# A convolution's weights arrive turned and early, and its 64-wide groups are spread over the four quadrants of the array

## The chip, the core and the metric

The kernel runs on one core of a Trainium2 chip. TensorE (PE) multiplies matrices and writes PSUM; VectorE (DVE), ScalarE (ACT) and GpSimd (POOL) do elementwise work, POOL only in SBUF; SyncE (SP) starts most DMA transfers. Each engine works through its own list of instructions in order, and they wait for each other by semaphores. The metric is the device time of one execution in microseconds (us).

## The reference, cut to what matters

Two layers, each an attention `s` and a gated network `g`, with `x = x + s * g`. The change is in the first layer, on 2 x 1024 tokens of 512 channels.

```
xn = layernorm(x)
# gate: g = silu(layernorm(relu(xn@up)**2 @ down + routed(xn)) * gamma + beta)
qkv = xn @ w_qkv.T                      # q 1024, k 256, v 256 channels
q = conv(q, qc1_w, qc1_b, groups=16)    # causal, 3 taps, 64 channels a group
k = conv(k, kc1_w, kc1_b, groups=4)     # the same, 4 groups
q = conv(q, qc2_w, qc2_b, groups=1);  k = conv(k, kc2_w, kc2_b, groups=1)
q += 0.5 * mean over heads of k_pre;    k += 0.5 * mean over heads of q_pre
... l2norm, rope, softmax attention, w_o
```

In the "first convolution" an output channel reads only the 64 channels of its own group, at three token positions.

## The kernel before, in words

The program is a row of phases, and between two phases all engines meet at a barrier.

**Gate phase** (names `a_`): four chunks of 512 tokens. Of each chunk DVE normalises x, PE transposes it to xnT, SP stores xnT to memory, PE makes the hidden, latent and output products, DVE and POOL do the second layernorm, ACT does the silu and stores g. Into a large buffer that is free at that time (`conv_in`) SP also loads the weights of the next phase as they lie in memory; the grouped ones go into blocks of 128x128 that POOL has zeroed (L280).

**Preparation** (a block of its own, L434 to L526): PE transposes 90 blocks of 128x128 weights (L450), ACT and DVE copy them to `b_wT`, `b_c1T`, `b_kc1T`, `b_kc2T`. ACT and DVE also measure the weights (sums of squares and of magnitudes, L474 to L496) for a bound on the size of the convolved q, from which a scale is worked out (L502 to L514), and DVE sums the weights over heads (`b_mean`, `b_meanT`, L520, L525). All this ends before the next block starts.

**Projection phase** (names `b_`, from L540): four rounds (2 batches x 2 halves of 512 tokens), each of 25 units. A unit is a group of matmuls into one of five PSUM banks, which ACT (even units) or DVE (odd units) empties ("takes"). Units 0 to 9 make q and k (4 matmuls of 128x512 each, L624). Units 10 to 19 are the first convolution, 8 for q and 2 for k: three matmuls, one a tap, with a 128x128 weight block in which two 64x64 groups stand on the diagonal and the rest is zero (L629). Then 2 units of v, one of the means, 2 of the second convolution of k. The q units are taken with scale and bias to one of two buffers `b_convs`, from which POOL makes a high and a low half-precision part in `conv_in` (L609, L611); a take waits until POOL is done with the buffer of two units before. The matmuls are float32, and the trace shows two MATMUL records for each (one for a transpose).

The query phase (names `c_`) then begins with DVE reading weights (L1045).

Of the kernel before, what the change touches and what calls it, by code (L numbers as in the profile page):

```python
# [9 lines left out]
ALU = mybir.AluOpType  # L10
# [53 lines left out]
def gate_phase(nc, sem, dram, ident, half, weights):  # L64

    with ExitStack() as ctx:
# [6 lines left out]
        up = sb("up", [P, KD, INT])  # L73
        down = sb("down", [P, MI, D])
# [6 lines left out]
        x_in = sb("x_in", [P, TT, D])  # L81
# [10 lines left out]
        g_out = sb("g_out", [P, TT, D])  # L92
# [40 lines left out]

        UNITS = MI + ML + 1 + ML
# [5 lines left out]
        def _(sp):  # L140
            sp.dma_start(x_in[:], x_rows[0]).then_inc(x_loaded, 16)
            sp.dma_start(ident[:], dram["ident"]).then_inc(w_loaded, 16)
            sp.dma_start(up[:], dram["up_w"].rearrange("(k p) n -> p k n", p=P)).then_inc(w_loaded, 16)
# [3 lines left out]
            sp.dma_start(down[:], dram["down_w"].rearrange("(k p) n -> p k n", p=P)).then_inc(w2_loaded, 16)  # L147
# [3 lines left out]

            weights.load(sp)
            sp.wait_ge(weights.zeroed, 1)
            weights.load_pairs(sp)
# [5 lines left out]
            for c in range(NCH - 1):  # L160
                sp.wait_ge(xn_ready, c + 1)
                sp.dma_start(x_in[:], x_rows[ds(c + 1, 1)].rearrange("a p t d -> p (a t) d")).then_inc(x_loaded, 16)
                store(c)
            store(NCH - 1)
# [52 lines left out]
        def _(act):  # L217
# [25 lines left out]
            def silu(c):  # L243
                act.wait_ge(g_stored, 16 * (c + 1))
                for t in range(TT):
                    act.wait_ge(shifted, c * TT + t + 1)
                    act.activation(g_out[:, t, :], y[:, t, :], ACT.Silu).then_inc(g_ready, 1)
                act.wait_ge(g_ready, (c + 2) * TT)
                act.dma_start(g_rows[ds(c, 1)].rearrange("a p t d -> p (a t) d"), g_out[:]).then_inc(g_stored, 16)
# [10 lines left out]
        def _(pool):  # L260
# [19 lines left out]
            pool.memset(weights.pairs, 0.0).then_inc(weights.zeroed, 1)  # L280
# [7 lines left out]
        def _(dve):  # L288
# [20 lines left out]
            def finish(c):  # L309
# [16 lines left out]
                for t in range(TT):  # L326
# [8 lines left out]
                for t in range(TT):  # L335
                    dve.tensor_scalar(y[:, t, :], y[:, t, :], mv2[:, t, 0:1], rstd2[:, t:t + 1],
                                      ALU.subtract, ALU.mult).then_inc(yn_ready, 1)

# [7 lines left out]
class ProjectionWeights:  # L346


    def __init__(self, dram, sem, space):
        flat = space[:].rearrange("p a m b n -> p (a m b n)").bitcast(F32)  # L350
        NO = (LAT + 2 * KVD) // P
        ends = [NO * D, (MQ + MK) * P * TAPS, MK * KVD * TAPS]
        at = [sum(ends[:i]) for i in range(4)]
        self.dram = dram
        self.rows = flat[:, at[0]:at[1]].rearrange("p (o d) -> p o d", d=D)
        self.pairs = flat[:, at[1]:at[2]].rearrange("p (m i a) -> p m i a", i=P, a=TAPS)
        self.dense = flat[:, at[2]:at[3]].rearrange("p (o i a) -> p o i a", i=KVD, a=TAPS)
        self.loaded = sem("b_w_loaded")
        self.conv_loaded = sem("b_conv_loaded")
        self.zeroed = sem("b_zeroed")  # L360

    def load(self, sp):
        sp.dma_start(self.rows, self.dram["w_qkv"].rearrange("(o p) d -> p o d", p=P)).then_inc(self.loaded, 16)
        sp.dma_start(self.dense.rearrange("p o i a -> p o (i a)"),
                     self.dram["kc2_w"].rearrange("(o p) i a -> p o (i a)", p=P)).then_inc(self.conv_loaded, 16)

    def load_pairs(self, sp):

        for g in range(2):
            lo = g * HD0  # L370
            for src, at, n in ((self.dram["qc1_w"], 0, MQ), (self.dram["kc1_w"], MQ, MK)):
                sp.dma_start(self.pairs[lo:lo + HD0, at:at + n, lo:lo + HD0, :].rearrange("p m i a -> p m (i a)"),
                             src.rearrange("(m g p) i a -> g p m (i a)", g=2, p=HD0)[g]).then_inc(self.conv_loaded, 16)


def project_phase(nc, sem, dram, ident, conv_in, weights, unscale, rows0, rows0_loaded):
# [7 lines left out]
    with ExitStack() as ctx:  # L384
# [3 lines left out]
        wT = sb("wT", [P, KD, LAT + 2 * KVD])  # L388
        meanT = sb("meanT", [P, 2, KD, P])
        mean = sb("mean", [P, 2, KD, HD0])  # L390
        c1T = sb("c1T", [P, MQ * TAPS, P])
        kc1T = sb("kc1T", [P, MK * TAPS, P])
        kc2T = sb("kc2T", [P, MK * TAPS, KVD])
        bias = sb("bias", [P, MQ + 2 * MK])
        scale = sb("scale", [P, 1])
        scaled_bias = sb("scaled_bias", [P, MQ])

        rows, pairs, dense = weights.rows, weights.pairs, weights.dense
        turned = sem("b_turned")
        out_act = sem("b_out_act")  # L400
        out_dve = sem("b_out_dve")
        mean_summed = sem("b_mean_summed")


        NO = (LAT + 2 * KVD) // P
        with ExitStack() as prep:
            magnitude = prep.enter_context(nc.sbuf_tensor("b_magnitude", [P, MQ, P * TAPS], F32))
            squares = prep.enter_context(nc.sbuf_tensor("b_squares", [P, MQ, D], F32))
            sums = prep.enter_context(nc.sbuf_tensor("b_sums", [P, 2, MQ], F32))
            most = prep.enter_context(nc.sbuf_tensor("b_most", [P, 3], F32))  # L410
            most_all = prep.enter_context(nc.sbuf_tensor("b_most_all", [P, 3], F32))
            peak = prep.enter_context(nc.sbuf_tensor("b_peak", [3, 1], F32))
            peaks = prep.enter_context(nc.sbuf_tensor("b_peaks", [3, 3], F32))
            ones = prep.enter_context(nc.sbuf_tensor("b_ones", [3, P], F32))
            root = prep.enter_context(nc.sbuf_tensor("b_root", [P, 2], F32))
            size = prep.enter_context(nc.sbuf_tensor("b_size", [P, MQ], F32))
            ps_w = prep.enter_context(nc.psum_tensor("b_ps_w", [P, P], F32))
            PIECES = tuple(range(4, 4 + 2 * MQ, 4))
            set_up, measured, bound_step = sem("b_set_up"), sem("b_measured"), sem("b_bound_step")
            peak_done, rooted = sem("b_peak_done"), sem("b_rooted")  # L420
            ps = [prep.enter_context(nc.psum_tensor(f"b_psw{i}", [P, CH], F32)) for i in range(4)]

            groups = []
            for o in range(NO):
                groups.append(([rows[:, o, k * P:(k + 1) * P] for k in range(KD)], wT[:, :, o * P:(o + 1) * P]))
            for m in range(MQ + MK):
                to = c1T[:, m * TAPS:(m + 1) * TAPS, :] if m < MQ else kc1T[:, (m - MQ) * TAPS:(m - MQ + 1) * TAPS, :]
                groups.append(([pairs[:, m, :, a] for a in range(TAPS)], to))
            for o in range(MK):
                for i in range(MK):  # L430
                    groups.append(([dense[:, o, i * P:(i + 1) * P, a] for a in range(TAPS)],
                                   kc2T[:, i * TAPS:(i + 1) * TAPS, o * P:(o + 1) * P]))
            with nc.Block() as block:
                @block.sync  # L434
                def _(sp):
                    for name, at, n in (("qc1_b", 0, MQ), ("kc1_b", MQ, MK), ("kc2_b", MQ + MK, MK)):
                        sp.dma_start(bias[:, at:at + n], dram[name].rearrange("(m p) -> p m", p=P), allow_slow_non_contiguous=True)\
                          .then_inc(weights.conv_loaded, 16)

                @block.tensor  # L440
                def _(pe):
                    for n, (blocks, _) in enumerate(groups):
                        if n == 0:
                            pe.wait_ge(weights.loaded, 16)
                        if n == NO:
                            pe.wait_ge(weights.conv_loaded, 16 * 8)
                        if n >= 4:
# [12 lines left out]
                def _(pool):  # L460
                    pool.memset(ones[:], 1.0).then_inc(set_up, 1)
# [97 lines left out]
        def _(sp):  # L559
# [21 lines left out]
            for h in range(2):  # L581
                load(0, h)
# [2097 lines left out]
```

## Time and profile before

| | us |
|---|---|
| median of 3 runs (lowest, highest) | 2746.51 (2740.61, 2748.51) |
| profiled execution | 2742.68 |
| its span | 2740.9 |
| PE busy | 2390.5 (87%) |
| DVE / ACT / POOL busy | 1241.3 / 930.7 / 749.7 |

The span is what the instructions cover; the execution's own time is 1.8 us more. A share of busy time is a mean over stages that have different limits, so the stretches of time are read one by one.

### The profile page before, as it was taken

The numbers are of one execution on the slowest core, as the hardware profiler recorded it, in microseconds if no ns is written. First come the engines' busy times: TensorE is split into PE (matmuls) and PEld (weight loads), VectorE is DVE, ScalarE is ACT, GpSimd is POOL, SyncE is SP. The second block draws the span as 40 slices with busy tenths as digits, with TensorE's granted clock in tenths as the row PEclk, the third lists the DMA queues.
The fourth block names the chain that finished last, engine by engine and source line by source line (L and its number), as shares of the span: only waits on it lengthen the run. The fifth ranks groups of instructions, "written<-read, shape, count | busy, mean of one in ns | idle before, by whom it ended". The sixth has DMA issues, their size and how long they took to land. (4 is left out here: it accounts for less than half of the span.)

```text
span 2740.9 us, 45944 instructions
## 1 busy us (share of the span) xinstructions
PE 2390.5 (87%) x19342; PEld 1141.3 (42%) x19342; DVE 1241.3 (45%) x2609; ACT 930.7 (34%) x1616; POOL 749.7 (27%) x749
## 2 busy tenths in 40 slices
PE   7999939999978999999499996898648888888866
PEld 3444424444433444444155552444324444444333
DVE  2332151100143333331267774244568888888712
ACT  1111121001021111110177771122417777777730
POOL 0111011102225222222244441111334434434400
PEclk9999969999989999999799998899869999999988
DMA  6000010010033111000422212331294444444222
GB/s 222 31 31 31 16 69 12 23 35 20 16 121 92 46 39 39 16 16 16 131 91 85 86 59 103 131 125 63 84 183 71 69 70 79 78 77 69 41 98 92
DMA packets 128271, 190.32 MB, mean 69 GB/s; under 512 B 40833, under 2 KB 63105, under 8 KB 126529
## 3 DMA queue, kind: packets, MB, share of 16 engines
q1 hardware_dynamic: 125952, 183.20, 25.6%
q8 instruction: 152, 2.49, 0.4%
q10 hardware_dynamic: 2112, 4.19, 0.4%
q14 instruction: 55, 0.44, 0.1%
HBM read 127.05 MB, written 60.29 MB: 68 GB/s over the span
## 5 line engine op out<-in xcount | busy, mean ns | idle before, releaser
L903 PE MATMUL c_ps_c<-conv_in,c_wT 128*128 128x512 f16 x2304 | 510.9, 382 | 2.5 <-DVE c_wT L1071 2.5
L2329 DVE TENSOR_REDUCE f_chunk_max<-f_ps_a 128x64 f32<-128x1024 f32 x320 | 319.5, 1032 | 63.2 <-PE f_ps_a L2073 40.8
L903 PEld LDWEIGHTS c_ps_c<-conv_in,c_wT 128*128 128x128 f16 x2304 | 223.2, 98 | 281.3 <-issue 16.8
L2200 ACT ACTIVATE f_probs<-f_ps_s 128x512 f32<-128x512 f32 x576 | 305.4, 603 | 99.1 <-PE f_ps_s L2112 46.3
L2073 PE MATMUL f_ps_a<-f_ka,f_qa 128*32 128x512 bf16 (+3 forms) x3072 | 199.6, 339 | 57.7 <-DVE f_chunk_max L2329 25.1
L2104 PE MATMUL f_ps_s<-f_qs,f_ks 128*32 128x512 bf16 x2304 | 208.5, 383 | 23.7 <-ACT f_qs L2191 14.6
L1344 ACT ACTIVATE d_probs<-d_ps_s,d_shift 128x512 f32<-128x512 f32 (+3 forms) x384 | 196.4, 583 | 82.6 <-PE d_ps_s L1283 72.3
L2126 PE MATMUL f_ps_o<-f_probs,f_v 128*32 128x512 f32 (+3 forms) x1536 | 150.7, 490 | 25.8 <-ACT f_probs L2200 25.7
L624 PE MATMUL b_ps<-b_xb,b_wT 128*128 128x512 f32 x320 | 139.9, 597 | 17.9 <-DMA b_xb<-xnT 17.9
L1278 PE MATMUL d_ps_s<-conv_in 128*64 128x512 f16 (+3 forms) x768 | 125.6, 329 | 27.1 <-DMA d_temp<-in_key_temp 27.1
L1294 PE MATMUL d_ps_o<-d_probs,conv_in 128*64 128x512 f32 (+3 forms) x768 | 146.0, 488 | 0.0
L2073 PEld LDWEIGHTS f_ps_a<-f_ka,f_qa 128*32 128x32 bf16 x3072 | 71.4, 97 | 178.4 <-DVE f_chunk_max L2329 66.3
L2191 ACT ACTIVATE f_qs<-f_ps_s 32x512 bf16<-32x512 f32 x192 | 112.6, 586 | 91.5 <-PE f_ps_s L2087 87.4
L1595 PE MATMUL e_ps_s<-e_oT,conv_in 128*128 128x512 f32 x256 | 116.4, 617 | 28.3 <-DMA conv_in<-in_x 17.2
L2269 POOL TENSOR_SCALAR f_absent<-f_rest 128x576 f32<-128x576 f32 x32 | 54.3, 1696 | 306.9 <-DVE f_rest L2346 182.8
L1411 DVE RECIPROCAL d_inverse<-d_ps_n 128x1024 f32<-128x1024 f32 x16 | 104.9, 6558 | 44.7 <-PE d_ps_n L1305 44.7
L1283 PE MATMUL d_ps_s<-conv_in 128*64 128x512 f16 (+3 forms) x384 | 124.5, 329 | 0.0
L1282 PE MATMUL d_ps_s<-conv_in 128*64 128x512 f16 (+3 forms) x384 | 124.5, 328 | 0.0
L207 PE MATMUL a_ps_d<-a_down,a_hidden 128*128 128x512 f32 x256 | 112.5, 592 | 0.0
L1036 DVE SCALAR_TENSOR_TENSOR c_raw<-c_ps_c,c_w_unscale,c_offset 128x512 f32<-128x512 f32 x32 | 24.0, 750 | 195.2 <-PE c_ps_c L903 195.2
L189 PE MATMUL a_ps_m<-a_xnT,a_up 128*128 128x512 f32 x256 | 110.8, 593 | 1.8 <-ACT a_relu L236 1.8
L1004 POOL TENSOR_TENSOR c_turned<-c_raw,c_cos 128x1024 f32<-128x1024 f32 x18 | 42.3, 2350 | 239.3 <-DVE c_swapped L1080 239.3
(263 smaller groups left out, 3680.8 us busy)
## 6 DMA issues: line engine op xcount, KB each, us to landing
f_qa<-qk SPq DMA_DIRECT2D x96, 128.0 KB, 3.8
f_qs<-qk SPq DMA_DIRECT2D x96, 128.0 KB, 4.4
conv_in<-q_parts SPq DMA_DIRECT2D x8, 1024.0 KB, 5.3
o0T<-d_stage SPq DMA_DIRECT2D x16, 512.0 KB, 2.6
conv_in<-o0T SPq DMA_DIRECT2D x4, 2048.0 KB, 10.3
qk<-e_part SPq DMA_DIRECT2D x12, 640.0 KB, 4.9
rows<-in_qc_w SPq DMA_DIRECT2D x4, 1536.0 KB, 7.6
c_rows<-in_qc_w SPq DMA_DIRECT2D x4, 1536.0 KB, 8.0
```

The lines of the kernel that those rows point to most:

```text
L624: last = pe.matmul(out[:], wT[:, k, u * P:(u + 1) * P], x[:, k, 1:], start=(k == 0), stop=(k == KD - 1))
L903: last = pe.matmul(ps_c[n % 2][:], wT[m % 2][:, w, i * TAPS + a, :], conv_in[:, x, i, b, h * CH + a:h * CH + a + CH], start=(i == 0 and a ...
L1278: pe.matmul(out[sides[e], lo - low:], k_high[b][:, keys[e]], q[b][:, h, lo:hi], start=True, stop=False)
L1282: pe.matmul(out[sides[0], lo - low:], k_low[b][:, keys[0]], q[b][:, h, lo:hi], start=False, stop=True)
L1283: pe.matmul(out[sides[1], lo - low:], k_low[b][:, keys[1]], q[b][:, h, lo:hi], start=False, stop=True)\
L1294: last = pe.matmul(ps_o[a * HD0:(a + 1) * HD0, lo:hi], v[b][:, kt, :], probs[n % RING][a][:, lo:hi], start=(kt == 0), stop=((kt + 1) * P = ...
L1344: act.activation(probs[n % RING][SCORES[c][1]][:, lo:hi], ps_s[c % BANKS][:, lo - hi + CH:], ACT.Exp, bias=shift[:, 0:1], scale=HD0 ** -0. ...
L2073: last = pe.matmul(out[side(e), h, 0:w], qa[u][:, 2 * p + h, side(e, qt * P)], ka[u][:, kh * CH:kh * CH + w], start=True, stop=not last_keys)
L2104: last = pe.matmul(out[side(e), :], ks[u][:, side(e, kt * P)], qs[u][version][:, :, at:at + P], start=True, stop=not (masked or part))
L2126: last = pe.matmul(ps_o[2 * HD1 * h:2 * HD1 * (h + 1), lo - half * CH:], v[u][:, kt, :], probs[m % HELD][:, h, lo - half * CH:], start=(kt ...
L2200: act.activation(probs[m % HELD][:, :, at:at + P], bank_of["s", i, n][:].rearrange("p (h n) -> p h n", n=P), ACT.Exp, scale=HD1 ** -0.5).t ...
L2329: dve.tensor_reduce(chunk_max[:, qt - 2, :, at:at + w // CHUNK], src.rearrange("p h (c k) -> p h c k", k=CHUNK), AX.X, ALU.max).then_inc(a ...
```

## The change

What it does:

1. The weights come from memory already transposed (`w_qkvT`, `qc1_wT`, `kc1_wT`, `kc2_wT`, laid out with the inputs). SP loads them, and the rows and taps that are only measured, behind the second chunk of x in the gate phase, into buffers of their own; the gate's `up`, `down` and `x_in` move to `conv_in` to make room, `g_out` to `rows0`. The memset of the pair blocks is gone.
2. The preparation block is gone. ACT and DVE measure the weights at the start of the projection phase, and the steps to the scale, the head sums and the means stand between DVE's takes of the first round.
3. The tokens of the first batch are loaded into `b_xb` in the gate phase.
4. In the gate phase each `bn_stats` of y follows its tile; in the last chunk DVE does gamma and beta of the last two tiles instead of POOL.
5. First convolutions: each 128-channel unit is split in two groups (rows 0 to 63, 64 to 127) by two halves of 256 tokens. The first half goes to the same side of bank `b_ps`, the second half crosses to the other side of a second bank `b_ps_x`, so that the four 64x64 weight positions of the array are all used. The take becomes three instructions: the straight bank, and each side of the crossed bank back to its own rows.

The core of the diff:

```diff
 def load(self, sp):
-    sp.dma_start(self.rows, self.dram["w_qkv"]...)
...
+    sp.dma_start(self.wT[:]..., dram["w_qkvT"]).then_inc(self.loaded, 16)
+    sp.dma_start(self.c1T[:]..., dram["qc1_wT"]).then_inc(self.loaded, 16)
+    sp.dma_start(self.kc1T[:]..., dram["kc1_wT"]).then_inc(self.loaded, 16)
+    sp.dma_start(self.kc2T[:]..., dram["kc2_wT"]).then_inc(self.loaded, 16)
+    sp.dma_start(self.rows, dram["w_qkv"][0:LAT]...).then_inc(self.rows_loaded, 16)
+    sp.dma_start(self.taps, dram["qc1_w"]...).then_inc(self.rows_loaded, 16)
...
     dve.bn_stats(stats2[:, t, :], y[:, t, :]).then_inc(stats2_done, 1)
...
+if c == NCH - 1:
+    for t in range(TT - LAST_DVE, TT):
+        dve.wait_ge(yn_ready, c * TT + t + 1)
+        dve.tensor_tensor(y[:, t, :], y[:, t, :], gamma[:], ALU.mult).then_inc(yn_ready, 1)
+        ...
+        dve.tensor_tensor(y[:, t, :], y[:, t, :], beta[:], ALU.add).then_inc(dve_shifted, 1)
...
     pe.wait_ge(*taken(n, of + m))
+    pe.wait_ge(*(taken(n, u - 2) if u >= C0 + 2 else taken(n - 1, u + V0 - C0 - 2)))
+    banks = out, ps_x[(u - C0) % 2]
     for a in range(TAPS):
-        last = pe.matmul(out[:], wgt[:, m * TAPS + a, :], src[:, m, lo + a:lo + a + CH],
-                         start=(a == 0), stop=(a == TAPS - 1))
+        for crossed in range(2):
+            at = crossed * HALF
+            for g in range(2):
+                rows_of, cols_of = half_of(g), half_of(1 - g if crossed else g)
+                last = pe.matmul(banks[crossed][cols_of, 0:HALF], wgt[rows_of, m * TAPS + a, :],
+                                 src[rows_of, m, lo + a + at:lo + a + at + HALF], ...)
...
+def crossed_take(engine, to, src, across, straight, crossed, factor):
+    for at, rows_of, from_rows, ps_in, added in ((0, slice(0, P), slice(0, P), src, straight),
+                                                 (HALF, slice(HD0, P), slice(0, HD0), across, crossed),
+                                                 (HALF, slice(0, HD0), slice(HD0, P), across, crossed)):
+        out, bank = to[rows_of, at:at + HALF], ps_in[from_rows, 0:HALF]
+        ...
```

PE's list from the end of the gate phase through the first round; `b_psw` are the banks of the transposes. Before:

```order
L450 MATMUL b_psw<-ident,conv_in 128x128 x90
L454 MATMUL b_ps_w<-ident,b_most 3x128
L457 MATMUL b_ps_w<-b_peaks,b_ones 128x3
L433 UNCONDITIONAL_BRANCH
L613 UNCONDITIONAL_BRANCH
L624 MATMUL b_ps<-b_xb,b_wT 128x512 x40
L629 MATMUL b_ps<-b_q_pre,b_c1T 128x512 x24
L629 MATMUL b_ps<-b_k_pre,b_kc1T 128x512 x6
L636 MATMUL b_ps<-b_wT,b_xb 128x128 x32
```

After:

```order
L528 UNCONDITIONAL_BRANCH
L551 MATMUL b_ps<-b_xb,b_wT 128x512 x20
L537 MATMUL b_ps_w<-ident,b_most 3x128
L551 MATMUL b_ps<-b_xb,b_wT 128x512 x8
L542 MATMUL b_ps_w<-b_peaks,b_ones 128x3
L551 MATMUL b_ps<-b_xb,b_wT 128x512 x12
L564 MATMUL b_ps<-b_q_pre,b_c1T 64x256 x2
L564 MATMUL b_ps_x<-b_q_pre,b_c1T 64x256 x2
L564 MATMUL b_ps<-b_q_pre,b_c1T 64x256 x2
L564 MATMUL b_ps_x<-b_q_pre,b_c1T 64x256 x2
```

The transposes and the block between are gone; the two small products of the bound stand between units 4 and 7; each tap of a unit is now four 64x256 products, two to each bank.

DVE's list in the first round of the projection phase. Before, the sums come first, in the preparation block:

```order
L520 TENSOR_REDUCE b_mean<-b_wT 128x64 x8
L525 TENSOR_SCALAR b_meanT<-b_mean 128x4x64 x4
L433 UNCONDITIONAL_BRANCH
L696 UNCONDITIONAL_BRANCH
L685 COPY b_q_pre<-b_ps 128x512 x4
L685 COPY b_k_pre<-b_ps 128x512
L675 TENSOR_SCALAR b_convs<-b_ps,b_scale,b_scaled_bias 128x512 x4
```

After:

```order
L642 COPY b_k_pre<-b_ps 128x512
L697 TENSOR_REDUCE b_mean<-b_wT 128x64 x4
L613 TENSOR_SCALAR b_convs<-b_ps,b_scale,b_scaled_bias 128x256
L613 TENSOR_SCALAR b_convs<-b_ps_x,b_scale,b_scaled_crossed 64x256 x2
L697 TENSOR_REDUCE b_mean<-b_wT 128x64 x2
L613 TENSOR_SCALAR b_convs<-b_ps,b_scale,b_scaled_bias 128x256
L613 TENSOR_SCALAR b_convs<-b_ps_x,b_scale,b_scaled_crossed 64x256 x2
L697 TENSOR_REDUCE b_mean<-b_wT 128x64 x2
L613 TENSOR_SCALAR b_convs<-b_ps,b_scale,b_scaled_bias 128x256
L613 TENSOR_SCALAR b_convs<-b_ps_x,b_scale,b_scaled_crossed 64x256 x2
L704 TENSOR_SCALAR b_meanT<-b_mean 128x4x64 x4
```

The eight sums and the means have moved between the takes of the convolution units, and a take is three instructions.

SP's list in the gate phase. Before (`conv_in` is the buffer that holds the raw weights):

```order
L363 DMA conv_in<-in_w_qkv 128x12x512
L364 DMA conv_in<-in_kc_w 128x2x768
L372 DMA conv_in<-in_qc_w 64x8x192
L372 DMA conv_in<-in_kc_w 64x2x192
L372 DMA conv_in<-in_qc_w 64x8x192
L372 DMA conv_in<-in_kc_w 64x2x192
L162 DMA a_x_in<-in_x 128x4x512
L158 DMA xnT<-a_xnT 128x4x512
```

After:

```order
L157 DMA conv_in<-in_x 128x4x512
L387 DMA b_wT<-in_w_qkvT 128x6144
L388 DMA b_c1T<-in_qc_wT 128x1536
L389 DMA b_kc1T<-in_kc_wT 128x384
L390 DMA b_kc2T<-in_kc_wT 128x1536
L391 DMA conv_in<-in_w_qkv 128x8x512
L392 DMA conv_in<-in_qc_w 128x8x192
L394 DMA b_bias<-in_qc_b 128x8x1
L394 DMA b_bias<-in_kc_b 128x2x1 x2
L398 DMA b_bias_crossed<-in_qc_b 64x8x1 x2
L398 DMA b_bias_crossed<-in_kc_b 64x2x1 x2
L153 DMA xnT<-a_xnT 128x4x512
```

The second chunk of x (here L157) now stands ahead of the weights.

## Rows read from the trace of the kernel before

**Rows 1.** Stretches of time: PE, PEld, DVE, ACT, POOL busy (count), PE clock, DMA.

```profile
342.50:402.80 60.30, 14.13 (x94) 12.49 (x95) 34.84 (x57) 15.74 (x29) 12.56 (x17) 0.66 0.13 40
402.80:755.80 353.00, 352.98 (x1008) 171.44 (x1008) 35.55 (x48) 33.96 (x51) 55.43 (x64) 1.00 0.08 27
```

**Rows 2.** Instructions in order of time (start, length), start of the gate phase.

```profile
10.24 3.30 POOL L280 MEMSET conv_in<- 128x3840 f32 x1
10.33 4.86 DVE L305 TENSOR_SCALAR a_xn<-a_x_in,a_mv,a_rstd 128x512 f32<-128x512 f32 x4 [1.23 <-POOL a_rstd L268]
...
43.57 1.92 DVE L305 TENSOR_SCALAR a_xn<-a_x_in,a_mv,a_rstd 128x512 f32<-128x512 f32 x4 [1.19 <-POOL a_rstd L268]
...
46.83 1.55 PE L189 MATMUL a_ps_m<-a_xnT,a_up 128*128 128x512 f32 x3 [1.79 <-ACT a_relu L236]
```

**Rows 3.** The same view, end of the gate phase.

```profile
343.93 2.46 DVE L328 BATCH_NORM_STATS2 a_stats<-a_y 128x6 f32<-128x512 f32 x4
...
348.01 3.80 DVE L336 TENSOR_SCALAR a_y<-a_y,a_mv,a_rstd 128x512 f32<-128x512 f32 x4 [1.13 <-POOL a_rstd L272]
...
358.13 1.26 POOL L277 TENSOR_TENSOR a_y<-a_y,a_beta 128x512 f32<-128x512 f32 x1
359.43 0.63 ACT L247 ACTIVATE a_g_out<-a_y 128x512 f32<-128x512 f32 x1 [1.93 <-POOL a_y L277]
...
364.86 0.37 SPq L437 DMA_DIRECT2D b_bias<-in_qc_b  x1
```

**Rows 4.** The same view, preparation block and start of the projection phase.

```profile
364.90 5.50 PE L450 MATMUL b_psw<-ident,conv_in 128*128 128x128 f32 x32 [22.47 <-PEq L66]
...
386.67 9.14 DVE L520 TENSOR_REDUCE b_mean<-b_wT 128x64 f32<-128x256 f32 x8
...
397.68 0.92 SPq L568 DMA_DIRECT2D b_xb<-xnT  x2
...
402.82 2.04 PE L624 MATMUL b_ps<-b_xb,b_wT 128*128 128x512 f32 x2 [17.88 <-DMA b_xb<-xnT]
```

**Rows 5.** Groups by line and shape, PE in the projection phase.

```profile
L629 PE MATMUL b_ps<-b_q_pre,b_c1T 128*128 128x512 f32 x192 | 83.1, 592 | 0.0
L629 PE MATMUL b_ps<-b_k_pre,b_kc1T 128*128 128x512 f32 x48 | 21.3, 592 | 0.0
```

**Rows 6.** Instructions in order of time, two units of the first convolution.

```profile
449.43 0.81 DVE L675 TENSOR_SCALAR b_convs<-b_ps,b_scale,b_scaled_bias 128x512 f32<-128x512 f32 x1 [4.34 <-PE b_ps L629]
...
450.30 0.61 POOL L609 CAST conv_in<-b_convs 128x512 f16<-128x512 f32 x1 [0.83 <-DVE b_convs L675]
...
450.99 1.09 POOL L611 TENSOR_TENSOR conv_in<-b_convs,conv_in 128x512 f16<-128x512 f32 x1
...
452.00 0.78 ACT L674 ACTIVATE b_convs<-b_ps,b_scaled_bias,b_scale 128x512 f32<-128x512 f32 x1 [4.37 <-PE b_ps L629]
```

**Rows 7.** The same view, float32 products in column tiles of 64 and of 32.

```profile
1383.71 1.94 PE L1294 MATMUL d_ps_o<-d_probs,conv_in 128*64 128x512 f32 x8
...
2107.30 1.03 PE L2126 MATMUL f_ps_o<-f_probs,f_v 128*32 128x512 f32 x8
```

**Rows 8.** Weight loads of the 64-wide tiles, by shape.

```profile
L1294 PEld LDWEIGHTS d_ps_o<-d_probs,conv_in 128*64 128x64 f32 x8 | 0.5, 136 | 1.1 <-issue 0.6 <-ACT d_o_raw L1328 0.5
```

**Rows 9.** Groups by line and shape, ACT and DVE in the preparation block.

```profile
L490 DVE TENSOR_REDUCE b_sums<-b_squares 128x2 f32<-128x1024 f32 x4 | 4.8, 1210 | 0.0
L499 DVE COPY b_wT<-b_psw 128x512 f32<-128x512 f32 x6 | 4.0, 686 | 16.4 <-PE b_psw L450 16.4
...
L499 DVE COPY b_c1T<-b_psw 128x384 f32<-128x384 f32 x4 | 2.1, 547 | 0.0
...
L479 ACT ACTIVATE b_wT<-b_psw 128x512 f32<-128x512 f32 x6 | 3.3, 596 | 7.1 <-PE b_psw L450 7.1
L479 ACT ACTIVATE b_c1T<-b_psw 128x384 f32<-128x384 f32 x4 | 1.8, 520 | 0.0
...
L520 DVE TENSOR_REDUCE b_mean<-b_wT 128x64 f32<-128x1024 f32 x4 | 7.2, 1855 | 0.0
```

More of the change, by code:

```diff
@@ L161, in _ @@
                 sp.wait_ge(xn_ready, c + 1)
-                sp.dma_start(x_in[:], x_rows[ds(c + 1, 1)].rearrange("a p t d -> p (a t) d")).then_inc(x_loaded, 16)
+                sp.dma_start(x_in, x_rows[ds(c + 1, 1)].rearrange("a p t d -> p (a t) d")).then_inc(x_loaded, 16)
+                if c == 0:
+                    weights.load(sp)
                 store(c)
+            sp.wait_ge(xnT_stored, 16 * 3)
+            sp.wait_ge(weights.x_padded, 1)
+            for h in range(2):
+                weights.load_tokens(sp, 0, h)
             store(NCH - 1)
@@ L279, in _ @@
             norm_x(0)
-            pool.memset(weights.pairs, 0.0).then_inc(weights.zeroed, 1)
+            pool.memset(weights.xb[0][:, :, 0:1], 0.0).then_inc(weights.x_padded, 1)
             pool.wait_ge(w2_loaded, 64)
@@ L367, in load_pairs @@
[L367 to L373, printed above, removed]
+        dram = self.dram
+        sp.dma_start(self.wT[:].rearrange("p k o -> p (k o)"), dram["w_qkvT"]).then_inc(self.loaded, 16)
@@ L529, in project_phase @@
-        xb = [sb(f"xb{i}", [P, KD, CH + 1]) for i in range(2)]
+        scaled_crossed = sb("scaled_crossed", [P, MQ])
+        bias_crossed = weights.bias_crossed
+        HALF = CH // 2
+        sums = sb("sums", [P, 2, MQ])
+        most = sb("most", [P, 3])
+        most_all = sb("most_all", [P, 3])
+        peak = sb("peak", [3, 1])
+        peaks = sb("peaks", [3, 3])
+        ones = sb("ones", [3, P])
+        root = sb("root", [P, 2])
+        size = sb("size", [P, MQ])
+        ps_w = ctx.enter_context(nc.psum_tensor("b_ps_w", [P, P], F32))
@@ L534, in project_phase @@
         convs = [sb(f"convs{i}", [P, CH]) for i in range(2)]
+        ps_x = [ctx.enter_context(nc.psum_tensor(f"b_ps_x{i}", [P, CH], F32)) for i in range(2)]
         UNITS, RING = MQ + MK + MQ + MK + 2 + 1 + MK, 5
@@ L542, in project_phase @@
         low_ready = sem("b_low_ready")
-        x_loaded = [sem(f"b_x_loaded{i}") for i in range(2)]
         made = sem("b_made")
@@ L690, in _ @@
             primed(act, took_act, N_ACT)
+            act.wait_ge(weights.rows_loaded, 16 * 9)
+            for x in range(PIECES):
+                tiles = slice(x * PER, (x + 1) * PER)
+                act.activation(taps[:, tiles, :], taps[:, tiles, :], ACT.Abs)
+                act.activation(size[:, tiles], bias[:, tiles], ACT.Abs)
+                act.activation(rows[:, tiles, :], rows[:, tiles, :], ACT.Square).then_inc(measured, 1)
             for b in range(B):
@@ L698, in _, with measure @@
             primed(dve, took_dve, N_DVE)
+            def measure():
+                for x in range(PIECES):
+                    tiles = slice(x * PER, (x + 1) * PER)
+                    dve.wait_ge(measured, x + 1)
+                    dve.tensor_reduce(sums[:, 0, tiles], rows[:, tiles, :], AX.X, ALU.add)
+                    last = dve.tensor_reduce(sums[:, 1, tiles], taps[:, tiles, :], AX.X, ALU.add)
+                last.then_inc(bound_step, 1)
+                dve.wait_ge(bound_step, 1)
+                dve.tensor_reduce(most[:, 0:2], sums[:], AX.X, ALU.max)
+                dve.tensor_reduce(most[:, 2:3], size[:], AX.X, ALU.max).then_inc(bound_step, 1)
@@ new lines, in sum_heads, with means @@
+            def sum_heads(n, k):
+                at, heads = ((LAT, KV0), (0, H0))[n]
+                dve.tensor_reduce(mean[:, n, k, :], wT[:, k, at:at + heads * HD0].rearrange("p (h c) -> p c h", c=HD0),
+                                  AX.X, ALU.add).then_inc(mean_summed, 1)
+            def means():
+                dve.wait_ge(mean_summed, 2 * KD)
+                for n, heads in enumerate((KV0, H0)):
+                    for copy in range(2):
+                        dve.tensor_scalar(meanT[:, n, :, copy * HD0:(copy + 1) * HD0], mean[:, n, :, :], 0.5 / heads,
+                                          None, ALU.mult).then_inc(mean_ready, 1)
@@ L699, in _ @@
+            dve.wait_ge(weights.loaded, 64)
+            measure()
             for b in range(B):
```

316 lines of the change are left out of this document (147 added, 169 removed).

## The prediction

> **What bounds the kernel now.** I read the table of stretches first, since the change ends at 755.8 us and what follows is untouched. Between 342.50 and 402.80 PE is busy 14.1 of 60.3 us; between 402.80 and 755.80 it is busy 352.98 of 353.00 at full clock (1.00), while DVE, ACT and POOL have 36, 34 and 55 us of work [rows 1]. So two different limits stand in the changed part: first a serial tail and preparation in which PE waits, then a projection phase in which PE is the only bound. The query phase starts from the end of the projection phase and has no other source, so what is gained before it should be gained whole.
>
> Next I read the instructions in order of time around the gap. PE's list ends at 342.4. DVE adds, takes the statistics of all four tiles in one go, normalises in 3.80 us, POOL's eight gamma and beta steps run to 359.4, ACT's last silu ends at 360.06, and its store and the barrier take until 364.86 [rows 3]. The preparation block then runs from 364.9 to the end of the head sums at 395.8 and the small means behind them; tokens are asked for at 397.68, and PE starts at 402.82 [rows 4]. Last, the groups by shape: the first convolution is 192 + 48 = 240 records of which one unit holds six, so 40 units, ten a round; its groups are busy 83.1 + 21.3 us [rows 5], which is 104.4 / 240 = 0.435 us a record with the groups' tails; without them I take 0.428, thus 2.57 a unit, 25.7 us a round, 102.8 in all.
>
> **Start of the gate phase: 2.8 us off.** POOL's 3.30 us memset lies beside DVE's four normalisations, which take 4.86 us there and 1.92 us in the next chunk [rows 2]. The memset goes, so up to 2.9 us come free; but PE also waits for the gate's own weights, which no edit hurries, and I take 1.0 (bounds 0 and 2.9). PE idles 1.79 us at 46.83 because DVE was kept by the late second chunk of x [rows 2], whose load now stands ahead of the weights: 1.8 (bounds 0 and 1.8). SP's later store of xnT waits behind twelve more transfers, but is next needed a chunk later (342.5 / 4 = 86 us).
>
> **Tail of the gate phase: 6.2 us off.** Three of four statistics, 3/4 of 2.46 = 1.85, move under PE's work. DVE's normalisation then ends at 351.8 - 1.85 = 349.96, and four products of its own follow: at 0.69 each (a copy of the same size is 686 ns [rows 9]) they end at 352.7, at twice their price beside POOL (the scaling steps are 0.95 each at the tail [rows 3] against 0.48 alone [rows 2]) at 355.5. POOL's four steps, at about 1.3 each [rows 3] from the first normalised tile at 346.8, are done by 352.4. With 0.63 for the silu the tail ends at 353.4 to 356.1 instead of 360.06: 6.7 to 4.0 off, and since POOL overlaps only the first part I take 6.2.
>
> **Preparation: 37.9 us off.** The block and the load behind it are 402.8 - 364.9 = 37.9 us [rows 4]. In their place PE starts at the barrier, with tokens and weights that arrived hundreds of us before. What moves under PE: DVE's measuring (4.8 us for the squares [rows 9], somewhat less for the taps, in step with ACT, which feeds it) runs during the first three units; five banks are free, so PE does not wait before its sixth unit at 17 us. The scale must be ready for the first convolution take, 34 us in: nothing waits. The two small products in PE's list come after their inputs. If this cover failed, the bound is the whole DVE chain, 10 us.
>
> **First convolutions: 33.9 us off.** The term that matters, and the trace shows no 64x64 tile. Its nearest rows are column tiles: eight float32 records of 512 columns, in two tiles of 64, take 1.94 us, in four tiles of 32 take 1.03 [rows 7]. Less the modelled tail of 0.16 these are 1.78 and 0.87, against 8 x 0.428 = 3.4 in one tile: two and four streams run side by side at full rate, float32 too. So four quadrants should hold four streams: 24 records of 256 columns, 0.214 each, by four, is 1.28 us a unit. Weight loads of 64 columns take 0.136 [rows 8], less than a pass of 0.214, so they stay hidden. Bounds: 1.28 (four at once), 2.57 (two at once), 5.14 (one by one).
>
> At 1.28 PE is no longer the bound. POOL needs 0.61 + 1.09 and about 0.06 between, 1.76 us a unit [rows 6]. A take is three instructions where it was one of 0.78 (ACT) or 0.81 (DVE) [rows 6]. Both engines show sizes: 128 columns fewer save 686 - 547 = 139 ns on DVE and 76 ns on ACT [rows 9]; 256 columns then cost about 0.53 on DVE and 0.56 to 0.63 on ACT, and with the overlap of neighbours (0.1) three take 1.4 to 1.7. I take 1.5. Chain of a round: unit 0 is made at 1.28 + 0.23 (the tail of 592 - 428 = 164 ns [rows 5] and a semaphore), taken at 3.0, then POOL follows at 1.76 a unit; take 7 waits for POOL's unit 5, 3.0 + 6 x 1.76 = 13.6, ends at 15.1, and only then may PE do unit 9: 16.5 us a round against 25.7. In the first round DVE has two sums of 1.855 [rows 9] behind take 1 and two behind take 3, each pair pushing the next take past POOL's pace by about 1.5: 19.4. Together 3 x 16.5 + 19.4 = 68.9, and 102.8 - 68.9 = 33.9. If POOL beside DVE's writes slows to 2.3 a unit, a round is 19.8 and the gain 23.5; at 2.57 for PE it is 0; one by one it is a loss of 102.8.
>
> The PSUM rule of the Trainium skill ("TensorEngine Tiling (Array Packing)", Gotcha 1: PSUM Pressure) speaks against this change: row tiles write to different banks and may not use the same bank at once. Here the two straight tiles lie on different rows and share one bank. By that rule pairs would exclude each other and two streams remain, which is the second case below; the trace has column tiles only and cannot say.
>
> **Sum.** 2.8 + 6.2 + 37.9 + 33.9 = 80.8, less 0.8 for the two small products and changes of tile shape, is 80. The profiled execution's own 2742.68 becomes 2662.7. It is 3.8 below the median of the runs shown, 2746.51, which becomes 2666.5.
>
> **Rivals.**
> *Two streams.* Row halves hinder each other, at the shared bank or because both feed the same output side, so a unit stays at 2.57. For it: no row tile anywhere in the trace. Against: at each output side the two row halves write different banks. Gain 80 - 33.9 = 46: 2700.
> *Convolutions paced higher.* POOL at 2.3 (DVE's writes beside it, as it is DVE that suffers in [rows 2, 3]), or PE's clock falls in a stage where it idles a quarter of the time: it was 0.66 in the gap [rows 1]. At half clock a unit is 2.57 again. Between 10 and 25 us of the 33.9 are lost: about 2684.
> *One stream.* Tiles of 64 by 64 run one after another (each change of row half waits for the array to empty). The place is PE's list of 240 products a round of 0.214 a record; a unit is 5.14, the phase grows by 102.8 and the start keeps its 46: 2746.5 - 46 + 102.8 = 2803, slower. It decides once a unit costs over 2.57 + 46/40 = 3.7 us. Against it: [rows 7].
> *The cover of the preparation fails*, because what DVE or ACT now does inside the first round holds up PE: 10 us back, 2676.
>
> **How the numbers follow.** Forecast 0.72, paced higher 0.09, cover fails 0.05, two streams 0.09, one stream 0.05. The forecast's own range is 2655 to 2676: the start terms give 5 either way, and takes of 1.4 to 1.7 move a round by less than 1. The range for all reaches up over two streams: 2652 to 2702, leaving the slow case and tails of some 0.1 out. A measurement of this kernel tells 0.3%, 8 us, from no change. All cases but one stream lie far below that: faster 0.94, same 0.01, slower 0.05.
>
> **What would show it.** The gate phase's last silu near 353.8 less 2.8, or about 351, and PE's first projection product near 356, with no DMA behind it. In a convolution unit 24 records of 256 columns start in fours, 0.214 apart; PE busy in the convolutions of a round is about 13 us of 16.5, and POOL is busy without a gap, while takes wait for POOL. The projection phase ends near 676 instead of 755.8, and everything behind it keeps its lengths. The forecast is wrong if starts come in twos, if the three instructions of a take last over 2 us, or if the projection phase ends later than 690.

## The result, and the profile after

| | before | after |
|---|---|---|
| median of the comparison | 2745.18 us | 2668.52 us (2666.57 to 2673.31) |
| ratio to before | | 0.9724, 95% interval 0.9705 to 0.9744 |
| span of the profiled execution | 2740.9 | 2665.8 |

The change saves 76.7 us. In the profiled spans it is 75.1, and three boundaries divide it: PE's end of the gate phase, the start of the projection phase, and its end.

| stretch | before | after | saved |
|---|---|---|---|
| to the end of PE's last gate product | 342.4 | 336.3 | 6.2 |
| from there to PE's first projection product | 60.4 | 18.0 | 42.4 |
| projection phase on PE | 353.4 | 327.2 | 26.2 |
| all that follows | 1984.7 | 1984.3 | 0.4 |

The stretches of time answer to [rows 1] (columns as there). First the gap and the whole phase, then the convolution stretches of the four rounds:

```profile
336.40:354.30 17.90, 0.00 (x1) 0.03 (x1) 10.96 (x16) 2.55 (x5) 6.83 (x5) 0.64 0.16 59
354.30:681.60 327.30, 311.06 (x1732) 164.11 (x1732) 71.50 (x118) 57.17 (x104) 55.99 (x71) 0.99 0.08 27
```

```profile
392.20:413.30 21.10, 14.21 (x242) 9.70 (x235) 18.99 (x26) 8.15 (x15) 13.75 (x16) 1.00 0.01 2
475.70:493.20 17.50, 14.70 (x242) 9.51 (x235) 7.16 (x14) 8.15 (x15) 13.37 (x16) 1.00 0.01 2
555.50:573.60 18.10, 14.70 (x242) 9.49 (x235) 7.17 (x14) 8.14 (x15) 13.88 (x16) 1.00 0.01 2
636.00:653.80 17.80, 14.72 (x242) 9.52 (x235) 7.18 (x14) 8.15 (x15) 13.87 (x16) 1.00 0.01 2
```

The gap has shrunk to the tail and the barrier. The phase, in which PE had no idle time, now has 16 us of it: in a convolution stretch PE is busy 14.7 of some 17.8 us, tails included, and in the first round DVE is busy 19.0 of 21.1. PE's granted clock is 1.00, its upper level of 2.4 GHz, in the four convolution stretches; it is 0.64 in the gap and 0.99 over the phase.

PE inside one unit, in order of time (start, length; the query began within the unit, whose earlier records are not shown). It answers to the column tiles of [rows 7]:

```profile
476.95 0.38 PE L564 MATMUL b_ps<-b_q_pre,b_c1T 64*64 64x256 f32 x2
476.96 0.38 PE L564 MATMUL b_ps_x<-b_q_pre,b_c1T 64*64 64x256 f32 x2
477.16 0.38 PE L564 MATMUL b_ps<-b_q_pre,b_c1T 64*64 64x256 f32 x2
477.18 0.38 PE L564 MATMUL b_ps_x<-b_q_pre,b_c1T 64*64 64x256 f32 x2
477.38 0.38 PE L564 MATMUL b_ps<-b_q_pre,b_c1T 64*64 64x256 f32 x2
```

Four records every 0.215 us: four streams, as the forecast had it. POOL and ACT some units later answer to [rows 6]:

```profile
644.57 0.61 POOL L524 CAST conv_in<-b_convs 128x512 f16<-128x512 f32 x1
645.26 1.15 POOL L526 TENSOR_TENSOR conv_in<-b_convs,conv_in 128x512 f16<-128x512 f32 x1
646.49 0.61 POOL L524 CAST conv_in<-b_convs 128x512 f16<-128x512 f32 x1
647.18 1.16 POOL L526 TENSOR_TENSOR conv_in<-b_convs,conv_in 128x512 f16<-128x512 f32 x1
648.28 0.61 POOL L524 CAST conv_in<-b_convs 128x512 f16<-128x512 f32 x1
```

```profile
644.72 0.56 ACT L608 ACTIVATE b_convs<-b_ps,b_scaled_bias,b_scale 128x256 f32<-128x256 f32 x1 [2.01 <-POOL conv_in L526]
645.30 1.13 ACT L608 ACTIVATE b_convs<-b_ps_x,b_scaled_crossed,b_scale 64x256 f32<-64x256 f32 x2
648.43 0.56 ACT L608 ACTIVATE b_convs<-b_ps,b_scaled_bias,b_scale 128x256 f32<-128x256 f32 x1 [2.00 <-POOL conv_in L526]
```

A take has become 1.70 us (0.56 + 1.13 and the step between) and waits for POOL, and POOL's next cast starts 0.1 us after the subtraction before it has ended: a pair of units every 3.71 us, 1.86 a unit, where PE alone would need 1.28.

The tail of the gate phase, in order of time, answers to [rows 3]:

```profile
342.39 1.32 POOL L281 TENSOR_TENSOR a_y<-a_y,a_beta 128x512 f32<-128x512 f32 x1
343.68 1.45 POOL L279 TENSOR_TENSOR a_y<-a_y,a_gamma 128x512 f32<-128x512 f32 x1
...
343.92 1.75 DVE L344 TENSOR_TENSOR a_y<-a_y,a_gamma 128x512 f32<-128x512 f32 x1
345.20 1.59 POOL L281 TENSOR_TENSOR a_y<-a_y,a_beta 128x512 f32<-128x512 f32 x1
345.71 1.63 DVE L346 TENSOR_TENSOR a_y<-a_y,a_beta 128x512 f32<-128x512 f32 x1
...
347.26 0.68 DVE L344 TENSOR_TENSOR a_y<-a_y,a_gamma 128x512 f32<-128x512 f32 x1
```

DVE's first two products cost 1.75 and 1.63 while POOL works, and 0.68 once POOL has stopped.

### The profile page after: what moved, and what is told of

Same layout as the page of the kernel before. It is cut to its first block and busy times, and to the rows that moved or that the text cites. A ratio compares the mean times of both kernels' runs of the same rounds, so it can differ in the third digit from the quotient of the medians.

```text
span 2665.8 us, 47249 instructions
## 1 busy us (share of the span) xinstructions
PE 2329.5 (87%) x19972; PEld 1119.5 (42%) x19972; DVE 1252.9 (47%) x2641; ACT 941.0 (35%) x1643; POOL 740.9 (28%) x744
## 3 DMA queue, kind: packets, MB, share of 16 engines
q8 instruction: 157, 2.57, 0.4%
## 5 line engine op out<-in xcount | busy, mean ns | idle before, releaser
L2098 PE MATMUL f_ps_a<-f_ka,f_qa 128*32 128x512 bf16 (+3 forms) x3072 | 199.2, 338 | 59.5 <-DVE f_chunk_max L2354 26.2
L2129 PE MATMUL f_ps_s<-f_qs,f_ks 128*32 128x512 bf16 x2304 | 208.4, 383 | 23.2 <-ACT f_qs L2216 14.6
L208 PE MATMUL a_ps_d<-conv_in,a_hidden 128*128 128x512 f32 x256 | 112.5, 592 | 0.0
L190 PE MATMUL a_ps_m<-a_xnT,conv_in 128*128 128x512 f32 x256 | 110.5, 592 | 0.0
```

The lines of the kernel that those rows point to most:

```text
L2098: last = pe.matmul(out[side(e), h, 0:w], qa[u][:, 2 * p + h, side(e, qt * P)], ka[u][:, kh * CH:kh * CH + w], start=True, stop=not last_keys)
L2129: last = pe.matmul(out[side(e), :], ks[u][:, side(e, kt * P)], qs[u][version][:, :, at:at + P], start=True, stop=not (masked or part))
```

## The experiments

All start from the changed kernel; their edits are shown shortened. Phase lengths are read on PE from their profiles, from the start of the first projection product to the end of the last product of the phase. Four of the eight kernels were timed once only, and these are read by their profiles.

**Two streams: only the tiles on the diagonal.** The medians of this and the changed kernel come from different comparisons with the kernel before.

```diff
-for crossed in range(2):
-    for g in range(2): ... banks[crossed][cols_of, 0:HALF] ...
+for g in range(2):
+    last = pe.matmul(out[half_of(g), :], wgt[half_of(g), m * TAPS + a, :], src[half_of(g), m, lo + a:lo + a + CH], ...)
```

(the take is one instruction again)

> The changed kernel, but the first convolution uses only the two tiles on the diagonal (rows and columns 0-63, rows and columns 64-127), each over all 512 tokens, and a unit is taken in one instruction as in the kernel before. All other parts of the change stay. Theory A (four quadrants hold four streams, two tiles hold two): a unit goes back to 2.57 us, a round's convolutions from 17.5-18.1 (21.1 in the first) to 25.7, so the projection phase grows by 28 us, 2668.5 to 2697. Theory B (two tiles on different rows that write one bank exclude each other, so four quadrants are really two streams and the gain came from elsewhere): a unit here costs 5.1 us, the phase grows by 131 us, 2800. The difference to the kernel before, under A, is what the start, the tail and the removed preparation are worth alone: 76.7 - 28 = 48 us.

Measured: 2700.26 us, ratio to before 0.9843 (0.9828 to 0.9859). The phase is 356.2 us against 327.2, a round's convolutions 25.9. Groups by shape, PE in that phase:

```profile
L561 PE MATMUL b_ps<-b_q_pre,b_c1T 64*64 64x512 f32 x384 | 83.3, 589 | 0.0
...
L561 PE MATMUL b_ps<-b_k_pre,b_kc1T 64*64 64x512 f32 x96 | 21.3, 588 | 0.0
```

That is 83.3 and 21.3 us, the groups of [rows 5] with twice the records: two tiles on different rows, writing one bank, run side by side. Theory A holds and B is out. The quadrants, with the dearer take that they need, are worth 29.0 us of the phase; the rest of the change alone beats the kernel before by 45 us. No run divides these 45 further; by the profiles the start, the tail and the removed preparation give 5.9 + 4.4 + 37.9 here, and the phase is 2.8 longer than before.

**Order of the quadrants: three taps in a row.**

```diff
-for a in range(TAPS):
-    for crossed in range(2):
-        for g in range(2): ...
+for crossed in range(2):
+    for g in range(2):
+        for a in range(TAPS): ...
```

> The changed kernel with the same 12 products a unit, but each quadrant does its three taps one after another before the next quadrant starts (in the change the quadrant changes with every product). Theory A (products start in list order, and one waits only for the tile it needs): three taps in one tile follow each other at 0.43 us, the next tile can start only when the third has started, so a unit costs about 4 x 0.86 + 0.43 = 3.9 us and a round 39, and the projection phase grows by some 85 us, to about 2750. Theory B (PE starts whatever tile is free, whatever the order of the list): a unit stays at 1.28 us and the time at 2668.

Measured: one time, 2690.84 us, the phase 350.4 (23.2 more). The second round's convolution stretch:

```profile
479.40:503.70 24.30, 24.30 (x242) 19.02 (x241) 7.21 (x13) 8.14 (x15) 13.58 (x16) 1.00 0.01 2
```

PE is busy throughout, 2.43 us a unit. Neither theory gave this number. In the middle of a unit, records of two banks start 0.06 to 0.16 apart, by turns, so about two tiles are at work (24 x 0.214 = 5.1 us of records in 2.43). By these records a waiting product does not block all that stand behind it, as A had it, and PE does not fill all four tiles whatever the order either, as B had it. The same 24 records cost 1.28 us in the one order and 2.43 in the other. That the order costs this much is shown; why it is two tiles and not one or four stays open.

**POOL's second step made cheaper.** The low part is no rounding error here, as the expectation says.

```diff
-pool.tensor_tensor(to(1), src, to(0), ALU.subtract).then_inc(low_ready, 1)
+pool.tensor_copy(to(1), src).then_inc(low_ready, 1)
```

> The changed kernel, but POOL's second step of a unit (high part subtracted from the value, 1.15 us) is a second plain cast (0.61 us), so the low half of the convolved q is not the rounding error any more. Theory A (the loop over POOL and the two buffers paces the convolution rounds: take 1.70 + POOL 1.84 + hand-offs per two units): with 1.30 a unit on POOL the rounds 2 to 4 go from 17.8 to 15.7, the first stays at 21 (DVE's sums pace it), together 6 us less, 2662. Theory B (the three-instruction takes and the second PSUM bank pace it, POOL only keeps up): rounds stay at 17.5 to 18.1, 2668.

Measured: 2663.68 us, ratio 0.9713 (0.9693 to 0.9733). That interval overlaps the changed kernel's, so the times alone show no difference; the profile does, with a phase of 322.7, 4.5 shorter. The later convolution stretches are 16.5 instead of 17.5 to 18.1, the first is 20.7 instead of 21.2. POOL had paced the later ones, so A holds in kind; but 1.3 us a round came instead of 2.1. In windows of 17.0 us over such a stretch POOL is busy only 9.7:

```profile
478.00:495.00 17.00, 14.52 (x246) 10.10 (x239) 7.65 (x15) 8.15 (x15) 9.66 (x16) 1.00 0.01 2
```

Behind POOL the next loop is close, and the waits show it. ACT's takes no longer wait for POOL but for PE, and PE waits for ACT's take:

```profile
482.82 0.57 ACT L608 ACTIVATE b_convs<-b_ps,b_scaled_bias,b_scale 128x256 f32<-128x256 f32 x1 [1.73 <-PE b_ps_x L564]
484.68 0.43 PE L564 MATMUL b_ps<-b_q_pre,b_c1T 64*64 64x256 f32 x2 [0.62 <-ACT b_convs L608]
486.26 0.56 ACT L608 ACTIVATE b_convs<-b_ps,b_scaled_bias,b_scale 128x256 f32<-128x256 f32 x1 [1.73 <-PE b_ps_x L564]
```

There are only two crossed banks, so unit m + 2 can start only when the take of unit m is done: a take of 1.70, PE's next unit of 1.28 in the bank that it frees, and the hand-offs make 3.44 a pair, against 3.71 with POOL's subtraction. A faster POOL alone does not return PE's idle time. Whether a third crossed bank or a shorter take would was not tried.

**Another order of the units.**

```diff
-for u in range(UNITS): unit(b, h, u)
+ORDER = [Q0..Q7, K0, C0, C1, K1, C2, C3, V0, C4, C5, V1, C6, C7, M0, KC0, KC1, K20, K21]
+for i in range(UNITS): unit(b, h, ORDER[i])
```

(bank, engine of the take and the waits go by the place in ORDER)

> The changed kernel with the units of a round in another order: 8 q units, then k0, two convolution units, k1, two convolution units, v0, two, v1, two, mean, two of k, and the two last of k. Nothing else. Theory A (in the convolution stretches of 17.5 to 21 us PE has 12.9 us of work, and what it lacks is only other work to do while takes and POOL catch up): PE has no idle time left in the projection phase, which shrinks by 4.9 + 4.9 + 5.2 + 8.3 = 23 us, to about 2646. Theory B (switching between 64x64 and 128x128 tiles drains the array, and takes of 1.7 us hold up the five banks): at least half of that is lost, 2657 or more.

Measured: 2654.68 us, ratio 0.9678 (0.9661 to 0.9695), so faster than the change, whose interval begins at 0.9705. The phase is 310.5, 16.7 shorter, not 23. First the whole phase, in which PE has no idle time left, then PE between two convolution pairs, in order of time:

```profile
360.40:670.80 310.40, 310.40 (x1732) 160.43 (x1732) 71.42 (x118) 57.10 (x103) 55.95 (x71) 0.99 0.08 29
```

```profile
479.91 0.38 PE L573 MATMUL b_ps_x<-b_q_pre,b_c1T 64*64 64x256 f32 x2
480.23 3.84 PE L580 MATMUL b_ps<-b_wT,b_xb 128*128 128x128 f32 x32
484.00 0.43 PE L573 MATMUL b_ps<-b_q_pre,b_c1T 64*64 64x256 f32 x2
```

32 records of 128 columns advance PE by 0.107 each, 3.43; from 479.91 + 0.215 to 484.00 there are 3.88. So going to another tile shape and back costs 0.45 us here, and there are five such returns a round where the change has one: 4 x 0.45 = 1.8 a round, 7 over four as an estimate, where 6 were missing. A's mechanism is right (PE only lacked other work), and of B the part on tile shapes is too.

**The start put back.**

```diff
+pool.memset(weights.xb[1][:, :, 0:480], 0.0)
-pool.memset(weights.xb[0][:, :, 0:1], 0.0)
+pool.memset(weights.xb[0][:, :, 0:480], 0.0)
+weights.load(sp)            # ahead of the loop over chunks
 for c in range(NCH - 1):
     sp.dma_start(x_in, ...)
-    if c == 0: weights.load(sp)
```

> The changed kernel with two things of the start of the gate phase put back: POOL clears 2 x 1920 columns (of the token buffers) beside DVE's first normalisations, and the second chunk of x is asked for behind the weights. Theory A (the start gained 1.5 us from the memset that is gone and 3.0 from the early second chunk; the other 1.7 of the 6.2 that the profiles show was a stretch at half clock behind the narrow gate products, which falls here or there by chance): PE's first transpose goes back from 13.9 to about 15.3, an idle stretch of 1.8 us before a hidden product comes back, the first chunk is about 4 us longer, and the number of half-clock stretches is one or two as it falls. Theory B (all 6.2 us belong to those two edits): the first chunk is 6 us longer.

Measured: one time, 2689.85 us. PE's first transpose is at 15.14 (13.87 in the change), as A said. The rest is in neither theory: the first chunk is 17 us longer (its narrow gate products start at 72.99 and not 56.20), so this run does not decide between 4 and 6 us. PE's wait, in order of time, and SP's list before it:

```profile
56.81 3.78 PE L189 MATMUL a_ps_m<-a_xnT,conv_in 128*128 128x512 f32 x4 [13.52 <-ACT a_relu L236]
```

```profile
16.67 12.93 SPq L392 DMA_DIRECT2D conv_in<-in_qc_w  x1
29.64 4.38 SPq L394 DMA_DIRECT2D b_bias<-in_qc_b  x1
34.06 5.73 SPq L394 DMA_DIRECT2D b_bias<-in_kc_b  x2
...
42.61 0.59 SPq L158 DMA_DIRECT2D conv_in<-in_x  x1
```

With the new, longer list of weights ahead of it, the second chunk of x is asked for at 42.6 and not at 13.1, and PE stands for 13.5 us, where it stood for 1.8 in the kernel before. The longer list was only free because that chunk was put in front of it. DVE's four normalisations beside the memsets take 4.89 us again, against 1.92 in the change. Half-clock stretches showed behind two of the four chunks' gate products.

**Gamma and beta on DVE alone.** The constant LAST_DVE is 4 instead of 2.

> The changed kernel, but in the last chunk DVE does gamma and beta of all four tiles and POOL none. Theory A (DVE and POOL slow each other: scaling 0.95 us a tile beside POOL against 0.48 alone, products 1.75 and 1.63 beside it against 0.69 alone): DVE needs 4 x 0.48 + 8 x 0.70 = 7.5 us where it now ends 8.5 us after it begins, so the store of g is issued about 1 us earlier after PE's last product (12.0 instead of 13.0). Theory B (DVE's products of three SBUF operands are slow in themselves, 1.7 each): 1.9 + 8 x 1.7 = 15.5, the store comes 7 us later.

Measured: one time, 2674.04 us; the tail itself is in the profile. From DVE's first step behind PE to the end of the last silu are 11.7 us (340.33 to 352.04) against 12.95. In order of time:

```profile
344.15 1.92 DVE L339 TENSOR_SCALAR a_y<-a_y,a_mv,a_rstd 128x512 f32<-128x512 f32 x4 [1.13 <-POOL a_rstd L276]
345.98 0.69 DVE L344 TENSOR_TENSOR a_y<-a_y,a_gamma 128x512 f32<-128x512 f32 x1
346.70 0.69 DVE L346 TENSOR_TENSOR a_y<-a_y,a_beta 128x512 f32<-128x512 f32 x1
```

Four scalings cost 1.92 instead of 3.81, and all eight products 0.69. Theory A holds: the two engines slow each other (POOL's steps, 1.26 alone in [rows 3], are 1.32 to 1.59 beside DVE in the change), and one alone is faster than both. PE starts the next phase 16.79 us after its last gate product instead of 18.03.

Most of that is lost again, though. PE's first 40 records of the phase, in the change and here:

```profile
354.30 19.47 PE L551 MATMUL b_ps<-b_xb,b_wT 128*128 128x512 f32 x40 [18.03 <-ACTq L55]
```

```profile
357.01 20.45 PE L551 MATMUL b_ps<-b_xb,b_wT 128*128 128x512 f32 x40 [16.79 <-ACTq L55]
```

PE starts at half clock after the gap; the granted clock is 0.50 from 354.3 to 358.3 in the change, and from 357.0 to 362.3 here; the other kernels with the 18 us gap take 19.2 to 19.8 for these records. The total time of this run is higher for two more reasons that are not the tail: slow stretches in two of its gate chunks, as told below, and one in the first convolution stretch, behind a wait of 2.70 for DVE:

```profile
412.00:414.00 2.00, 2.00 (x28) 1.26 (x24) 1.45 (x3) 0.00 (x0) 1.84 (x3) 0.50 0.00 0
```

**The head sums earlier.**

```diff
-u == 9: sum_heads(0, k) x4;  u in (11, 13): sum_heads(1, .) x2;  u == 15: means()
+u == 1, 3, 5, 7: sum_heads(...), and means() behind u == 7
```

> The changed kernel with DVE's head sums and means moved from behind its takes 9 to 15 to behind its takes 1 to 7 of the first round, where DVE idles some 6 us between two takes. Theory A (the first convolution stretch is 21.1 us instead of 17.5 to 18.1 because those sums hold up DVE's takes): it falls to about 17.8, the phase is 3.3 us shorter. Theory B (it is longer for another reason, such as the scale arriving late or POOL starting cold): it stays at 21.

Measured: one time, 2668.43 us, the phase 324.0, 3.2 shorter. The first convolution stretch:

```profile
395.80:413.40 17.60, 14.76 (x241) 9.47 (x240) 7.22 (x13) 8.16 (x15) 13.10 (x16) 1.00 0.01 2
```

17.6 instead of 21.1: theory A. The total does not show it, since that execution's gate phase ended 3.6 us later.

**Order, sums and tail together.**

> The interleaved order, with the early sums and with gamma and beta of the last chunk on DVE alone. Both rest on the two runs beside it. Theory A: the interleaved first round hid the sums already (it was 79.9 us, of which about 3 are the cold start and the two small products, against 77.0 for the others), so only the tail's 1 us is added: 2653.5. Theory B: the sums still cost there and the gain is 3 us more, 2651.

Measured: 2656.53 us, ratio 0.9668 (0.9652 to 0.9684), the phase 311.4. The intervals of this and of the interleaved kernel overlap widely: no difference can be told. That fits theory A, that the new order had hidden the sums already, but 1 us of tail is below what these runs resolve, and here too the gap is 16.79 us while the first 40 records take 20.05, against 19.16 in the interleaved kernel. The interleaved order is the version I would keep; what the tail on DVE is worth in the end is not shown.

## Why the prediction was right

The forecast of 2666.5 stands 2.0 us below the measured 2668.5. Its forecast case held. Two streams and one stream fell: 24 records take 1.28 us, in fours. Pacing at 2.3 us a unit on POOL fell: it is 1.86. The other half of that rival, a falling clock, did not show in this profile (1.00 in all four stretches); in one later run with the same phase (gamma and beta on DVE alone) it did, for some 3 us of the first round. The cover of the preparation held. The closeness of the two numbers is in part luck, as the terms show.

- **Preparation, 37.9.** Right: the gap lost 42.4, of which 37.9 is the block and its load and 4.4 the tail. The cover held: PE's sixth unit waited for nothing, and the scale was ready at 386.3, before the first convolution product at 391.9. What moved did cost something in the phase: the head sums and means are 3.6 us of the first convolution stretch (21.2 against 17.6 with the sums earlier), of which the forecast had 2.9.
- **Quadrants.** The step from column tiles to quadrants was the open one, and the price of 1.28 us a unit was met. The rule of the Trainium skill that was weighed ("TensorEngine Tiling (Array Packing)", Gotcha 1: PSUM Pressure) does not hold here as a cost: two row tiles that write different partitions of one bank ran side by side, 83.3 us for what took 83.1 in one tile. Two row tiles on the same partitions of one bank were not tried.
- **The round around it, mis-sized.** I forecast 16.5 us a later round and 19.4 for the first; they were 17.5, 18.1, 17.8 and 21.2, so that the term of 33.9 was 28.2. The mechanism, a chain of take and POOL, was right. The step that was off is above all the take: "256 columns then cost about 0.53 on DVE and 0.56 to 0.63 on ACT, and with the overlap of neighbours (0.1)". The prices were right (0.54 and 0.56), the overlap did not come, so three are 1.70 and not 1.5. POOL's subtraction was 1.15 instead of 1.09, and a unit on POOL 1.86 instead of 1.76. The forecast's own chain with the measured numbers, 1.5 + 1.70 + 6 x 1.86 + 1.70 + 1.3, gives 17.4. It was also tighter than forecast: two units on POOL take 3.7 us, and a buffer's own turn, a take of 1.70, its unit on POOL of 1.84 and 0.17 of hand-offs, takes 3.71 too. The run with two casts shows a third loop, over PE and the crossed banks, close behind. In the first round the means, 0.9 us in the preparation, took 2.2 while POOL worked.
- **Rest of the phase, a loss of 0.8.** It was 2.0: the phase is 26.2 shorter and its convolutions 28.2. The first 80 records of the phase take 37.6 us to the first convolution product (354.30 to 391.89) instead of 36.1, with the two small products among them and a slow start.
- **Tail, 6.2.** It was 4.4. The bound of 4.0 was the nearer end: DVE beside POOL pays 1.75 and 1.63 for products that cost 0.69 alone. I had the doubled price and weighted it too little. POOL's end at 352.4 is a slip (346.8 + 4 x 1.3 = 352.0) that changes nothing, since DVE ends later.
- **Start, 2.8.** It was 6.2 in the two profiles, above the bounds, which add to 4.7. (With the tail's, my bounds reach 5.0 below the two terms but only 2.4 above them, not "5 either way".) The first chunk's narrow gate products (8 columns) start 4.5 us earlier, at 56.20 instead of 60.66. Of that, 1.5 is the first transpose, which now waits for the gate's own weights (`a_expert`) until 13.87; 1.8 is the idle time that is gone; 1.0 is a shorter slow start in the first products, which varies from run to run. The other 1.7 is chance: behind the narrow products the granted clock falls to 0.50 for a few records in some chunks. Group rows of that step, the first chunk before and after:

```profile
L198 PE MATMUL a_ps_m<-a_latent,a_expert 128*128 128x512 f32 x8 | 5.4, 837 | 0.0
L193 PE MATMUL a_ps_m<-a_gate,a_xnT 128*128 128x8 f32 x30 | 3.5, 256 | 0.0
```

```profile
L199 PE MATMUL a_ps_m<-a_latent,a_expert 128*128 128x512 f32 x8 | 3.7, 602 | 0.0
L194 PE MATMUL a_ps_m<-a_gate,a_xnT 128*128 128x8 f32 x32 | 3.6, 253 | 0.0
```

The clock in that stretch of the first chunk before:

```profile
66.15:68.15 2.00, 2.00 (x4) 0.94 (x3) 0.00 (x0) 0.60 (x1) 0.00 (x0) 0.50 0.00 0
```

Before, two of four chunks had such a stretch, after, one. In the other runs whose gate phase has the changed kernel's code up to PE's end, PE ended it at 336.3, 336.6, 339.3, 339.7, 339.9, 340.2 and 342.3, by which chunks were hit and for how long. The change's own profile, at 336.3, is among the luckiest of the eight; their mean is 338.8. The kernel before has one profile only. By the rows that the edits explain the step is worth about 4.5, and the rest is luck.

So the errors are 5.7 too much (rounds), 1.8 too much (tail), 1.2 too much (rest of the phase) and 3.4 too little (start), about half of which is luck; 0.4 more came behind the phase. They cancelled in part: 80 forecast, 75.1 in the spans, 76.7 in the medians. That the forecast and the measured time lie only 2.0 apart owes something to the median before, too: the forecast starts from 2746.51, and that median came out at 2745.18 in the comparison.

## What to carry to other kernels

When small groups are spread over tiles of the array, count what empties the banks before counting the gain: here a unit got twice as fast on the array (2.57 to 1.28 us), its take went from one instruction to three, and 16.7 of some 23 us of time that PE then lacked work came back by giving it products of other units between pairs. Change the tile with every product; the same products grouped by tile lost 23.2 of the phase's 26.2 us of gain. And a list of transfers that moves to an early place is free only behind the transfer that the critical engine needs next.

## What the runs showed of the hardware

- Four 64x64 float32 tiles run at once: four records of 256 columns start every 0.215 us. Two on different rows, writing different partitions of one bank, run at once over 512 columns (83.3 us for 384 records). With three products of a tile in a row about two of four are at work (2.43 us a unit instead of 1.28).
- Changing from 64x64 tiles to the whole array and back cost PE 0.45 us around a unit of 32 records.
- Beside POOL's work in SBUF, DVE's scaling of a 128x512 float32 tile is 0.95 instead of 0.48 us and a product up to 1.75 instead of 0.69; beside a 3.3 us memset of POOL four scalings take 4.86 us instead of 1.92.
- Instructions on 64 partitions cost as much as on 128 (0.56 us on ACT and 0.54 on DVE for 256 columns), so crossing the halves back doubles the price of that half.
- A PE clock of 1.2 GHz behind narrow products came in one or two of four equal chunks, at 1.7 or 3.4 us each, and the gate phase of equal programs ended between 336.3 and 342.3 us.
